# Second attention as 32x32 head blocks, gated halves spread between divisions, router logits with stationary weights, last batch interleaved with the next layer norm

## What is computed

```
x = x + tanh(g_xattn[0]) * attention_0(ln(x), ctx, mask)      # softmax, 16 heads of 32
x = x + tanh(g_ffn[0])   * ffn_0(ln(x))                       # silu(gate)*up, 1408 wide
x = x + tanh(g_xattn[1]) * attention_1(ln(x), ctx)            # linear attention, gated
x = x + tanh(g_ffn[1])   * ffn_1(ln(x))                       # 16 experts, top 2, + shared

attention_1: phi(t) = t + 1 if t > 0 else exp(t)
  q = phi(ln_x @ Wq.T);  k, v = split(ctx @ Wkv.T);  k = phi(k)
  S = sum_s k[s] v[s]^T  (32 x 32 a head);  z = 1 / (q . sum_s k[s] + eps)
  out = ((q @ S) * z * sigmoid(ln_x @ Wg.T + bg)) @ Wo.T
ffn_1 router: scores = softmax(t @ gate_w.T); the two largest of 16 weight their experts
```

## Time and profile before

| | |
|---|---|
| median of 3 runs | 1012.65 us (1010.91 to 1013.94) |
| the profiled execution | 1014.06 us, of which 1012.4 are the span from the first to the last instruction |
| TensorE busy, mean granted clock | 956.3 us (94%), 0.974 |
| VectorE, ScalarE, GpSimd busy | 465.4, 275.9, 82.2 us |
| chain that ended last, by engine | PE 83%, DVE 8%, DMA 3%, ACT 2%, issue 2%, POOL 1% |

### The profile page before, as it was taken

The page is one execution under the profiler, slowest core; times in us unless marked ns, Lnnn a source line. Parts: engine busy times, 40 slices in busy tenths (PEclk is TensorE's granted clock), DMA queues, the critical chain, the costliest instruction groups (busy, mean ns, idle before and its releaser), DMA issues.

```text
span 1012.4 us, 17141 instructions
## 1 busy us (share of the span) xinstructions
PE 956.3 (94%) x7151; PEld 732.9 (72%) x7152; DVE 465.4 (46%) x751; ACT 275.9 (27%) x424; POOL 82.2 (8%) x111
## 2 busy tenths in 40 slices
PE   5999999999999999889999999989999989999991
PEld 5878788887878787679997447977996446566550
DVE  6664555454554465962220446977322311222224
ACT  4533333333333334232111114332210021121210
POOL 0000000000000010100000003120000502222111
PEclk9999999999999999879999999999799999999996
DMA  8100010010100020430003005513402317977726
GB/s 323 31 2 32 2 32 32 1 33 1 74 2 32 1 84 2 178 155 1 1 1 125 1 0 215 201 58 110 148 1 86 147 43 244 330 250 247 265 69 232
DMA packets 26770, 95.99 MB, mean 95 GB/s; under 512 B 3282, under 2 KB 4306, under 8 KB 23634
## 3 DMA queue, kind: packets, MB, share of 16 engines
q1 hardware_dynamic: 20354, 72.69, 20.2%
q0 software_dynamic: 6352, 22.35, 6.2%
HBM read 76.37 MB, written 18.66 MB: 94 GB/s over the span
## 4 chain that ended last, share of the span: by engine, by line
PE 83%; DVE 8%; DMA 3%; ACT 2%; issue 2%; POOL 1%; SPq 0%; POOLq 0%; DVEq 0%; ACTq 0%
PE ps L540 17%; PE ps L541 16%; PE ps L542 16%; PE ps L932 10%; PE ps L801 7%; PE ps L942 5%; PE ps L620 4%; PE ps L603 3%; PE ps L821 1%; POOL sorted_rows L1785 1%; PE ps L923 1%; DVE arena L1294 1%; DMA land_c<-in_ctx 1%; DVE stats L1282 1%; PE ps L949 1%
## 5 line engine op out<-in xcount | busy, mean ns | idle before, releaser
L540 PE MATMUL ps<-arena_r 128*125 128x512 f32 (+1 forms) x416 | 164.3, 395 | 4.2 <-DVE arena_r L1260 4.2
L541 PE MATMUL ps<-arena_r 128*125 128x512 f32 (+1 forms) x416 | 157.3, 378 | 0.0
L542 PE MATMUL ps<-arena_r 128*125 128x512 f32 (+1 forms) x416 | 157.1, 378 | 0.0
L540 PE MATMUL ps<-hT,arena_r 128*128 128x448 f32 (+1 forms) x368 | 138.2, 376 | 3.5 <-DVE hT L1301 3.3
L541 PE MATMUL ps<-hT,arena_r 128*128 128x448 f32 (+1 forms) x368 | 136.4, 371 | 0.0
L542 PE MATMUL ps<-hT,arena_r 128*128 128x448 f32 (+1 forms) x368 | 136.3, 370 | 0.0
L932 PE MATMUL ps<-arena 128*128 x336 | 103.1, 460 | 1.8 <-ACT arena L1216 1.0
L996 ACT ACTIVATE arena<-arena,mbias,mscale 125x448 f32<-125x448 f32 x96 | 66.1, 752 | 106.1 <-DVE arena L1382 106.1
L540 PEld LDWEIGHTS ps<-arena_r 128*125 128x125 f32 (+1 forms) x416 | 78.3, 188 | 21.9 <-DVE arena_r L1260 4.6
L542 PEld LDWEIGHTS ps<-arena_r 128*125 128x125 f32 (+1 forms) x416 | 78.2, 188 | 13.7
L932 PEld LDWEIGHTS ps<-arena 128*128 128x128 f32 x336 | 62.3, 190 | 33.3 <-issue 2.2
(11 more groups left out here) (197 smaller groups left out, 1172.6 us busy)
## 6 DMA issues: line engine op xcount, KB each, us to landing
arena<-in_e SPq DMA_DIRECT2D x16, 1408.0 KB, 6.8
arena<-in_e SPq DMA_DIRECT2D x16, 512.0 KB, 7.5
sorted_rows<-arena POOLq DMA_DIRECT2D x1, 7453.0 KB, 24.2
land_c<-in_ctx SPq DMA_DIRECT2D x8, 752.0 KB, 4.3
arena<-sorted_rows POOLq DMA_DIRECT2D x21, 257.0 KB, 5.4
land_w<-in_gu SPq DMA_DIRECT2D x8, 512.0 KB, 4.5
arena<-token_rows SPq DMA_DIRECT2D x14, 256.0 KB, 4.7
arena<-in_e SPq DMA_DIRECT2D x16, 192.0 KB, 9.6
```

The costliest lines, as they stand in the source:

```text
L540: mm(into, a[0], w[0], start=i == 0, stop=False)
L541: mm(into, a[0], w[1], start=False, stop=False)
L542: last = mm(into, a[1], w[0], start=False, stop=i == len(operands) - 1)
```

## The change

1. *Last batch.* All outputs of attention 0 go to bank 6, each waiting for the delta of the tile before. Outputs move forward in TensorE's list (tile 4 from behind the summary to the third score block), and the transposes of tiles 0 to 4 stand between mixes, values and summary; VectorE's and ScalarE's lists are reordered to match. In the last batch `k1` goes to a place of its own (`k1_last`), so x tiles 4 to 6 are reloaded after the seventh summary; gu0 chunks 6 to 8 are loaded after the eighth.
2. *Attention 1.* `attend` uses `kvc` and `ksr` by 32x32 blocks, 32 matmuls instead of 8, the four heads of a group in one bank at partitions 0, 32, 64, 96. Memsets and copies of `kvbd`, `ksbd` go; one ScalarE copy in FFN 0, chunk 4, makes `ksr`. sh2 is loaded without waiting for the attends.
3. *Gated halves.* Pieces 0 to 3 are split between the attends' divisions.
4. *Router.* The router weights (high and low side by side, 32 columns) are stationary and half of all tokens moves past them, sixteen matmuls of 448 columns; ScalarE copies the result (`lgT`), and seven matmuls with it as the stationary operand and `pair` (two stacked identities) moving bring it back to tokens and add both parts. VectorE's low half of shared chunk 1 moves behind the layer norm.

Banks of transposes and outputs, then SP's early reload:

```diff
-                return (0, 1, 2, 3, 1, 3, 1)[n - NT]
+                return (0, 1, 2, 3, 0, 1, 3)[n - NT]
-            return (6, 6, 6, 6, 5, 6, 4)[n] if n < NT else n % 2
+            return 6 if n < NT else n % 2
...
+            sp.wait_ge(kv_mm, B - 1)
+            sp.dma_start(x[:, RT_AT:NT, :], x_in.rearrange("(t p) d -> p t d", p=P)[:, RT_AT:NT, :]).then_inc(x_again, 16)
             sp.wait_ge(kT_mm, 4 * B)
```

TensorE's list, last batch:

```diff
             mix(b, 0)
             values_1(b, 0)
+            to_tokens(1, output_of_0)
             scores(b, 2)
             keys_1(b, 1)
-            to_tokens(1, output_of_0)
+            to_tokens(2, output_of_0)
             mix(b, 1)
             values_1(b, 1)
-            to_tokens(2, output_of_0)
+            to_tokens(3, output_of_0)
             scores(b, 3)
             keys_1(b, 2)
+            to_tokens(4, output_of_0)
+            pe.wait_ge(clipped, 4 * B)
+            ln_transposes(NT)
             mix(b, 2)
+            ln_transposes(NT + 1)
             values_1(b, 2)
-            to_tokens(3, output_of_0)
+            to_tokens(5, output_of_0)
+            ln_transposes(NT + 2)
             mix(b, 3)
+            ln_transposes(NT + 3)
             kv_summary(b)
-            to_tokens(4, output_of_0)
-            to_tokens(5, output_of_0)
-            pe.wait_ge(kv_sv, B)
+            ln_transposes(NT + 4)
             to_tokens(6, output_of_0)
-            pe.wait_ge(clipped, 4 * B)
-            for t in range(4):
-                ln_transposes(NT + t)
```

VectorE's list, last batch, the new order behind `clip(b, 3)` (the lines removed are the same calls, later):

```diff
+            feed_low(1, gu0[1])
             keys_1(b, 2)
+            residual(3)
+            delta(4)
+            ln_low(NT)
+            ln_norm(NT + 3)
+            residual(4)
+            ln_low(NT + 1)
+            ln_norm(NT + 4)
+            delta(5)
+            ln_low(NT + 2)
             normalise(b, 1)
+            heads_low(b)
+            ln_low(NT + 3)
+            residual(5)
             kv_save(b)
```

`attend` on TensorE:

```diff
-                for j, w in enumerate((kvbd, ksbd)):
+                for j, w in enumerate((kvc, ksr)):
                     for g in range(G):
-                        last = mm(ps[:, 2 * j + b % 2, g * S:(g + 1) * S], w[:, b * G + g, :],
-                                  qT[:, g, b * S:(b + 1) * S], start=True, stop=True)
+                        for h in range(HG):
+                            r = slice(h * HD, (h + 1) * HD)
+                            last = mm(ps[r, 2 * j + b % 2, g * S:(g + 1) * S], w[r, b * G + g, :],
+                                      qT[r, g, b * S:(b + 1) * S], start=True, stop=True)
```

The router on TensorE:

```diff
+                for k in range(KC):
+                    mm(into[0:2 * NE], gate_r[:, k, :, :].rearrange("p j e -> p (j e)"), piece(hT, k, n * HALF, HALF)[0],
+                       start=k == 0, stop=False)
+                    last = mm(into[0:NE], gate_r[:, k, 0, :], piece(hT, k, n * HALF, HALF)[1],
+                              start=False, stop=k == KC - 1)
...
             last_transposes(3)
             pe.wait_ge(y_sv, 3 * NT)
+            logits_T(0)
             pe.wait_ge(gu_low, MC + 2)
             gate_up(1, sh13[1], P, 0, 0)
             pe.wait_ge(ln_T, 4 * NT)
-            for t in range(NT):
-                last = product(ps[:, 1, t * NE:(t + 1) * NE],
-                               [(tok(hT, k, t), (gate_r[:, 0, k * NE:(k + 1) * NE], gate_r[:, 1, k * NE:(k + 1) * NE]))
-                                for k in range(KC)])
-            last.then_inc(lg_mm, 1)
+            logits_T(1)
             gate_up(0, sh13[0], P, 1, 0)
             gate_up(0, sh13[0], P, 1, 1).then_inc(ff_mm, 1)
+            pe.wait_ge(lgT_sv, 2)
+            for t in range(NT):
+                last = mm(ps[:, 1, t * NE:(t + 1) * NE], lgT[:, t * P:(t + 1) * P], pair[:], start=True, stop=True)
+            last.then_inc(lg_mm, 1)
             gate_up(1, sh13[1], P, 0, 1)
-            pe.wait_ge(lg_sv, 1)
-            gate_up(1, sh13[1], P, 1, 0)
-            gate_up(1, sh13[1], P, 1, 1).then_inc(ff_mm, 1)
+            gate_up(1, sh13[1], P, 1, 1)
+            pe.wait_ge(lg_max, 1)
+            gate_up(1, sh13[1], P, 1, 0).then_inc(ff_mm, 1)
```

VectorE's list, attention 1:

```diff
             for b in range(2, B):
                 attend(b)
-            for i in range(8):
+                for j in ((), (), (), (0,), (1, 2), ())[b - 2]:
+                    gated_low(j)
+            for i in range(3, 8):
                 gated_low(i)
```

VectorE's list, layer norm of FFN 1:

```diff
-                if t in (3, 4):
-                    feed_low(MC + t - 3, sh13[t - 3])
+                if t == 3:
+                    feed_low(MC, sh13[0])
             ln_norm(4 * NT - 1)
             ln_low(4 * NT - 2)
             ln_low(4 * NT - 1)
+            feed_low(MC + 1, sh13[1])
```

More of the change, by code:

```diff
@@ L215, in flamingo @@
         gT = at(28160, KC, TOK)
-        kvbd = at(31744, B * G, P)
-        ksbd = at(35840, B * G, P)
+        ksr = at(47040, B * G, HD)
         A_SH = 40192
@@ L464, in _ @@
             sp.wait_ge(v1_mm, 3 * B)
-            for m in range(2, 9):
+            for m in range(2, 6):
                 sp.dma_start(gu0[m][2], gu0_in[m]).then_inc(gu0_ld[m], 16)
             sp.wait_ge(kv_mm, B)
-            sp.dma_start(x[:, RT_AT:NT, :], x_in.rearrange("(t p) d -> p t d", p=P)[:, RT_AT:NT, :]).then_inc(x_again, 16)
+            for m in range(6, 9):
+                sp.dma_start(gu0[m][2], gu0_in[m]).then_inc(gu0_ld[m], 16)
             sp.wait_ge(ln_var, 2 * NT)
@@ L775, in _ @@
             gate_up(0, gu0[0], P, 0, 0)
+            ln_transposes(NT + 5)
+            pe.wait_ge(y_sv, NT)
             gate_up(0, gu0[0], P, 0, 1)
-            ln_transposes(NT + 4)
             pe.wait_ge(gu_low, 2)
+            pe.wait_ge(ln_T, NT + 5)
+            gate_up(1, gu0[1], P, 0, 0)
+            ln_transposes(NT + 6)
             gate_up(1, gu0[1], P, 0, 1)
-            ln_transposes(NT + 5)
-            ln_transposes(NT + 6)
-            gate_up(1, gu0[1], P, 0, 0)
+            pe.wait_ge(normed, 2 * B)
             pe.wait_ge(ln_T, 2 * NT)
@@ L1096, in _ @@
             keys_1(b, 0)
+            delta_std(0)
+            ln(NT)
             values_1(b, 0)
+            fn(warm[:, 0:1], eps[:], ACT.Exp)
+            feed_high(0, gu0[0], gu0_ld[0])
             exps(b, 2)
             keys_1(b, 1)
+            delta_std(1)
+            ln(NT + 1)
+            delta_std(2)
             values_1(b, 1)
-            delta_std(0)
-            fn(warm[:, 0:1], eps[:], ACT.Exp)
+            ln(NT + 2)
+            fn(warm[:, 1:2], eps[:], ACT.Exp)
+            feed_high(1, gu0[1], gu0_ld[1])
             exps(b, 3)
             keys_1(b, 2)
-            feed_high(0, gu0[0], gu0_ld[0])
-            delta_std(1)
-            delta_std(2)
-            ln(NT)
+            delta_std(3)
+            ln_save(NT)
+            ln(NT + 3)
+            ln_save(NT + 1)
+            delta_std(4)
             values_1(b, 2)
-            feed_high(1, gu0[1], gu0_ld[1])
-            ln(NT + 1)
+            ln(NT + 4)
+            ln_save(NT + 2)
             heads_save(b)
-            delta_std(3)
-            ln(NT + 2)
-            delta_std(4)
+            ln_save(NT + 3)
             delta_std(5)
-            ln(NT + 3)
-            for t in range(4):
-                ln_save(NT + t)
+            ln_save(NT + 4)
+            ln(NT + 5)
             delta_std(6)
-            for t in range(4, NT):
-                ln(NT + t)
-            for t in range(4, NT):
-                ln_save(NT + t)
+            ln_save(NT + 5)
+            ln(NT + 6)
+            ln_save(NT + 6)
             for m in range(MC):
@@ L1129, in _ @@
                 act.wait_ge(ff_mm, m + 1)
+                if m == 4:
+                    act.wait_ge(kv_sv, B)
+                    fn(ksr, ks[:].rearrange("p b g -> p (b g)").unsqueeze(2).broadcast_to([P, B * G, HD]),
+                       ACT.Copy).then_inc(ksr_set, 1)
                 if m >= 2:
@@ L1186, in _ @@
                    bias=cols[:, 8 + m:9 + m]).then_inc(g1_sv, 1)
-                if i >= 5:
-                    gated_high(i - 5)
-            for i in range(3, 8):
+                for j in ((), (), (), (0,), (1, 2), (3,), (), ())[i]:
+                    gated_high(j)
+            for i in range(4, 8):
                 gated_high(i)
@@ L1198, in _ @@
             ln_save(4 * NT - 1)
+            for n in range(2):
+                act.wait_ge(lg_mm, n + 1)
+                fn(lgT[:, n * HALF:(n + 1) * HALF], ps[0:2 * NE, 1 + 2 * n, 0:HALF], ACT.Copy).then_inc(lgT_sv, 1)
             act.wait_ge(lg_max, 1)
@@ L1472, in _ @@
             delta(0)
+            residual(0)
+            ln_norm(NT)
+            delta(1)
             clip(b, 2)
+            feed_low(0, gu0[0])
             keys_1(b, 1)
[L1475 removed]
+            residual(1)
+            ln_norm(NT + 1)
+            delta(2)
+            residual(2)
             normalise(b, 0)
[L1477 removed]
+            ln_norm(NT + 2)
+            delta(3)
             clip(b, 3)
[L1479 removed]
+            feed_low(1, gu0[1])
             keys_1(b, 2)
```

(8 more changed lines are left out.)

85 lines of the change are left out of this document (29 added, 56 removed).

## The result

The changed kernel takes 999.71 us (median of 4, 998.12 to 1000.16) against 1013.30 for the kernel before beside it: ratio 0.9869, interval 0.9850 to 0.9888, 13.3 us less. The forecast was 15.2 us less and 997.5 us, range 991.5 to 1006. The profiled execution took 999.32 us (span 997.7); before it was 1014.06 (1012.4).

What follows compares the result with a forecast made beforehand. TensorE, busy 94% of the span with clock dips, was taken as the bound, VectorE in the last batch. Terms -3.2 - 8.1 - 3.9 = -15.2 took 1014.06 to 998.9, or 997.5 beside the median; range 991.5 to 1006.

Steps and rivals of the forecast that it cites:

- Part 1, -3.2: Last batch of attention 0: merging it brings the second half of FFN 0 forward from 449.7 to 446.5, 3.2 us less.
- I add 2.5 us for the clock: Last batch: half clock behind the 5.7 us wait ahead of output 6 delays the product from 444.0 to 446.5.
- the walk: Last batch, both orders stepped engine by engine: new waits of 0.6, 1.0, 1.8 and 5.7 us, product at 444.0.
- VectorE, not TensorE, bounds the stretch: Last batch of attention 0: VectorE is the bound, and what is late next is `heads_low`.
- Part 2, -2.65 + 1.0: Attention 1: attend(0) starts 2.65 us earlier without memsets and copies; eight attends cost 0.12 us more each, 1.0 in all.
- the row of line 620: Attend: nearest profiled small matmuls, 48 in 1.29 us, 26.9 ns each, so 64 records take 1.72 us.
- Part 3, -4.95 - 1.5: Behind attention 1's gates, wait and slow start go, 4.95 us; moving a weight half out of the layer norm saves 1.5.
- part 4, -3.9: Router logits: gross 9.5 us saved, more than half lost to a new wait ahead of shared chunk 2; 3.9 net.
- A (serial tiles): Rival in attend: tiles run one after another, 6.2 instead of 1.79 us each, about 1032 us in all; chance 0.10.
- 0.429 x 112/512: Attend: a lone pass of 112 columns, scaled from line 801's 512-column records, takes 0.094 us.
- B (the last batch gives nothing): Rival in attention 0: the merged last batch gives nothing or loses, up to +1.5 us; 1002 or 1005 us; chance 0.15.
- C: Rival at the router: no wait ahead of shared chunk 2, so the gross 9.5 us comes; 992 us; chance 0.05.

Runs made afterwards that it cites:

- three pairs: Kernels with and without part 1: 0.9991 against the kernel before; 0.9869 against 0.9871; with two further edits 0.9798 against 0.9793.
- second profile of the same kernel: The changed kernel run and profiled again with nothing edited; 999.23 us, ratio 0.9862 to the kernel before.
- the reordered kernel: Changed kernel with early `hidden`, shared chunk 0's second half before chunk 1, and attention 0's last mix, normalisation and `heads_low` earlier; 990.79 us, 0.9772.
- part 2 alone: The kernel before with only the attention 1 change (attend from 32x32 blocks, no memsets and copies); 1012.74 us, ratio 0.9994.
- part 4 alone: The kernel before with only the router change (router weights stationary); 1008.08 us, ratio 0.9937.
- part 1 alone: The kernel before with only the last-batch change; 1012.98 us, ratio 0.9991.
- exchanged order: The changed kernel with attend's loops exchanged, so four successive 32x32 tiles lie in the same rows and columns; 1014.84 us, ratio 1.0025.

## Why the prediction came out as it did

The total (-15.2 forecast, -13.3 measured, -12.9 in the profile without the start) came out because segments B, C and D of the whole change did; what is missing of it lies in part 1. The parts by themselves did not give their terms: 0.9, 0.6, 2.0 and 6.4 us where the prediction has 3.2, 1.65, 6.45 and 3.9.

**Part 1, -3.2: wrong in size.** Measured in three pairs it is nothing, and two of them exclude 3.2 us. Two things were wrong. The step "I add 2.5 us for the clock" takes one loss behind one wait, but the loss differs between executions of one kernel: in the profiled one TensorE waited 2.07 us at 399.9, where the walk had 0.6, and ran the next 5 us at 0.66, about 1.7 us at most; in the second profile of the same kernel that clock loss is absent. And the walk priced FFN 0's matmuls the same on both sides, while in three profiles with this order they stand 0.2067 apart, which gives back 1.9 us. To the second half of FFN 0 the changed kernel's profile gained 1.76 us (449.68 to 446.09, less the 1.83 of the start). By segment A the old order has 218.4 to 219.8 (mean 219.2 of 6), the new 217.0 to 218.0 in the four profiles with the usual spacing and 220.0 to 220.4 in the three with the slow one (without the reordered kernel), 218.5 in the mean: 0.7 us for the part, and 1.9 where the spacing is the usual one. The reading that VectorE, not TensorE, bounds the stretch held: moving VectorE's last normalisation forward shortened A in the reordered kernel.

**Part 2, -2.65 + 1.0: right in the traces.** B gives -2.66 and C +0.62 for seven attends, 0.09 each; in timed runs of part 2 alone no gain is clear of noise. And the attend's 1.74 us lies on the row of line 620 from which it was taken (1.72). The rule that the prediction cites against this form ("TensorEngine Tiling (Array Packing)" of the Trainium skill, Restrictions and Gotchas: different row tiles can't access one PSUM bank at the same time) isn't borne out by these runs: the four heads' tiles are different row tiles in one bank, and their records start within 0.02 us of each other, one round every 96 ns. "PSUM — Partial Sum Buffer" of the Trainium skill, the four PSUM rules, which calls accumulation groups in different quadrants independent, is compatible with that, but it speaks of accumulation and not of time, so it didn't decide the question. What was missed is a benefit: beside the memsets the old kernel can lose another 3.4 us (part 4 alone, one profile of four).

**Part 3, -4.95 - 1.5, and part 4, -3.9: right together, not each.** D gives -10.9 for -10.35. The waits of 1.08 and 3.30 us and the clock behind the second came as worked out. But without part 4 the saving of part 3 goes into a 2.80 us wait and a longer half-clock stretch at the old logits, so the split between the two terms holds only in this order of adding them. There is some luck in the sum too. The old code's own D varies, 116.06, 117.63 and 117.31 in three profiles, since its half-clock stretch begins earlier in some; before's was the shortest. How that stretch lies in the kernel with part 1 alone (PE busy (count), PEclk):

```profile
705.00:710.00 5.00, 5.00 (x34) 1.00 1.03 375
710.00:715.00 5.00, 5.00 (x36) 0.75 1.05 359
715.00:720.00 5.00, 5.00 (x26) 0.50 0.57 199
720.00:725.00 5.00, 5.00 (x22) 0.50 0.00 0
725.00:730.00 5.00, 5.00 (x16) 0.54 0.00 0
```

In the earlier trace rows matmuls still took 0.11 us at 714.8; here the clock had fallen before 715, in a kernel that is 1.1 us ahead. Part 4 removes the stretch, so it saves more in such executions than in the one profiled before, which fits the 6.4 us of part 4 alone.

**The rivals.** A (serial tiles) did not occur. Its step "0.429 x 112/512", 94 ns for a lone pass, held: records of one place start 96 ns apart. The exchanged order was meant to make it occur and did so only in part, two tiles at a time instead of four: it cost some 16 us, not 34, and puts the kernel at the time of before. What fully serial tiles would cost has no run. B (the last batch gives nothing) is the one that happened, in its mild form, while the rest held. C was right in its size: with the wait removed the gain is 5.0 to 5.7 us for 5.6, and the kernel is at 992.7 for 992 forecast.

## What to carry to other kernels

When a product pays for a wait, look at what stands ahead of the releasing instruction in its engine's queue: moving one `hidden` ahead of a chain whose result TensorE needed only later gave 5 to 5.7 us, some two fifths of the whole change. Small tiles that share the array should be issued so that neighbours differ in rows and columns. Merging a stage in which another engine is the bound mostly moved the waits about here; a wait of over 3 us nearly always cost clock as well, one of 2 us only sometimes. And two profiles of one kernel can differ by 3 us in one stage, so a term of that size needs several.

## What the runs showed of the hardware

- Records of one 32x32 fp32 tile with 112 moving columns start 96 ns apart. Four tiles in different rows and columns, writing different quadrants of one bank, run at once (27 ns a record); in the exchanged order, with four tiles in a row in the same place, it is 60 ns a record.
- Matmuls of 448 columns, streamed without a wait at a granted clock of 1.00, stand 0.2027 us apart in some executions and 0.2067 in others of the same kernel, over 100 us at a time in FFN 0 and over 14 to 20 us in the shared FFN.
- A 128x512 norm on VectorE took 0.55 us without the memsets; the last two of attention 1's layer norm took 1.38 and 3.04 us in one profile and 5.31 and 1.45 us in another beside two 4096-word memsets on GpSimd.
- The same wait of TensorE, 2.07 us in the same code, was followed by a granted clock of 0.66 over 5 us in one execution and 1.00 in another.
